# Later places for the casts of the middle parts of the last two tiles in a fused attention kernel

## What is computed

```
q = (x @ wq).reshape(B, T, H, D)          # B=16, T=512, H=16, D=16
lat = x @ w_down
k = (lat @ wk_up).reshape(B, T, H, D)
v = (lat @ wv_up).reshape(B, T, H, D)
q = _apply_rope(q, cos, sin)
k = _apply_rope(k, cos, sin)
scores = jnp.einsum('bqhd,bkhd->bhqk', q, k) * scale
scores = jnp.where(allowed[None, None], scores, jnp.finfo(scores.dtype).min)
attn = jax.nn.softmax(scores, axis=-1)
out = jnp.einsum('bhqk,bkhd->bqhd', attn, v).reshape(B, T, E)
return out @ wo
```

## Time and profile before

| | |
|---|---|
| median of 3 runs | 1903.85 us |
| lowest, highest | 1903.59, 1912.81 us |
| the profiled execution, its own time | 1909.18 us |
| its span, first to last instruction | 1907.3 us |
| attention turns with the changed table | about 640 to 1290 us of the span |
| one full turn | 47.1 us |

### The profile page before, as it was taken

How to read it: one execution, slowest core, us unless ns; L and a number is a source line. 1 busy time by engine, 2 the same in 40 slices (tenths; PEclk the granted TensorE clock), 3 DMA queues, 4 the chain that set the end, 5 groups by cost and what they waited for, 6 DMA issues and landing times. The chain is left out here.

```text
span 1907.3 us, 32059 instructions
## 1 busy us (share of the span) xinstructions
PE 1791.9 (94%) x10553; PEld 1102.0 (58%) x10554; DVE 1311.0 (69%) x3400; ACT 1124.8 (59%) x2292; POOL 843.5 (44%) x923
## 2 busy tenths in 40 slices
PE   6999999999957799999999999999799999989997
PEld 3666666777733355555555555555456666667776
DVE  4777776566638577777777777777277777756664
ACT  5777775125424667777777777777477777721111
POOL 1111101777746666566655555550011111147776
PEclk9999999999977899999999999999899999999999
DMA  2424341999933333333333333332222433249996
GB/s 77 128 84 142 95 131 56 264 258 258 260 77 94 95 100 103 101 102 101 102 101 102 101 101 102 90 90 58 66 86 73 129 108 123 80 143 261 263 259 145
DMA packets 192287, 243.72 MB, mean 128 GB/s; under 512 B 17559, under 2 KB 159607, under 8 KB 192126
## 3 DMA queue, kind: packets, MB, share of 16 engines
q1 hardware_dynamic: 166286, 202.62, 35.0%
q0 software_dynamic: 24576, 37.77, 10.3%
q10 hardware_dynamic: 1264, 1.31, 0.2%
HBM read 126.65 MB, written 63.86 MB: 100 GB/s over the span
## 5 line engine op out<-in xcount | busy, mean ns | idle before, releaser
L1403 DVE TENSOR_REDUCE a_smax<-a_p_ring 128x1 f32<-128x512 f32 (+2 forms) x768 | 355.2, 506 | 134.1 <-PE a_p_ring L1494 128.5
L1302 ACT ACTIVATE a_probs<-a_p_ring 128x512 f32<-128x512 f32 x640 | 368.2, 607 | 109.0 <-PE a_p_ring L1506 107.7
L1494 PE MATMUL a_p_ring<-p_ks,p_qs 100*128 100x512 bf16 (+3 forms) x1024 | 246.6, 307 | 16.3 <-ACT a_smaxT L1339 5.5
L1506 PE MATMUL a_p_ring<-p_qs,p_ks 103*128 103x512 bf16 (+3 forms) x1024 | 243.4, 304 | 6.7 <-ACT a_probs L1302 5.8
L50 POOL TENSOR_TENSOR f_rstd<-f_mv,eps 128x4 f32<-128x4 f32 x31 | 14.8, 478 | 497.8 <-DVE f_mv L44 495.5
L676 ACT ACTIVATE e_silu<-e_p_up 128x176 f32<-128x176 f32 x128 | 40.6, 318 | 313.0 <-PE e_p_up L768 313.0
L519 PE MATMUL f_p_up<-f_xnT,ws1T 128*128 128x512 f32 x384 | 187.4, 611 | 1.1 <-ACT f_xnT L300 1.1
L1522 PE MATMUL a_p_out<-a_probs,p_v 128*32 128x512 f32 (+3 forms) x2048 | 177.6, 448 | 6.1 <-ACT a_probs L1302 6.1
L561 PE MATMUL f_p_z<-ws2T,f_hidden 128*128 128x256 f32 (+1 forms) x768 | 180.6, 384 | 0.7 <-DVE f_hidden L397 0.7
L137 POOL DMA_INDIRECT h_got<-rows,slot_token x128 | 125.8, 983 | 123.9 <-DVE slot_token L496 83.0
L519 PE MATMUL f_p_up<-f_xnT,ws3T 128*128 128x512 f32 x384 | 180.5, 592 | 0.0
(11 more groups left out here) (171 smaller groups left out, 3613.8 us busy)
## 6 DMA issues: line engine op xcount, KB each, us to landing
h_w<-w_in SPq DMA_DIRECT2D x128, 352.0 KB
p_qs<-a_parts SPq DMA_DIRECT2D x192, 128.0 KB, 2.4
p_ks<-a_parts SPq DMA_DIRECT2D x192, 128.0 KB, 2.4
h_w<-w_in SPq DMA_DIRECT2D x128, 176.0 KB
rows<-first_row SPq DMA_DIRECT2D x16, 640.0 KB, 6.4
rows<-f_row SPq DMA_DIRECT2D x16, 640.0 KB, 6.6
x<-x_in SPq DMA_DIRECT2D x16, 512.0 KB, 5.7
acc<-x SPq DMA_DIRECT2D x16, 512.0 KB, 3.3
```

Source lines behind the costliest of these rows:

```text
L1302: nc.scalar.activation(to[:], p_score[s][:], ACT.Exp, scale=SCALE).then_inc(score_free[s], 1)
L1403: ins = nc.vector.tensor_reduce(smax[:, t, 4 * g + h:4 * g + h + 1], p_score[s][:, at:at + length], AX.X, ALU.max)
L1494: ins = nc.tensor.matmul(p_score[s][:, at:at + length], qs[1 - u][0:SR + MASK, 4 * g + h, t * P:(t + 1) * P], ks[1 - u][0:SR + MASK, 4 * g ...
L1506: ins = nc.tensor.matmul(p_score[s][:, at:at + length], ks[u][0:SR + MASK + TOP, 4 * g + h, t * P:(t + 1) * P], qs[u][0:SR + MASK + TOP, 4 ...
```

## The change

Two numbers of the table `PROJECT` are different; no instruction is added or taken away.

```diff
-           (0.61, ("HIGH", 2)), (0.69, ("HIGH", 3)), (0.74, ("SPLIT", 2)), (0.765, ("SPLIT", 3))]
+           (0.61, ("HIGH", 2)), (0.69, ("HIGH", 3)), (0.80, ("SPLIT", 2)), (0.855, ("SPLIT", 3))]
```

## The result

| | before | with the change |
|---|---|---|
| median of 7 runs | 1903.85 us | 1897.39 us |
| lowest, highest | 1903.48, 1912.81 | 1893.53, 1901.79 |
| ratio to before, 95% interval | | 0.9957, 0.9940 to 0.9974 |
| profiled execution, its span | 1907.3 us | 1891.7 us |
| a full turn, mean of six | 47.19 us | 46.60 us |

The kernel became faster by 0.43% by the ratio (0.34% by the medians), and the interval leaves out no change. The forecast was 1896.4 us, 0.39% less, in a range of 1890 to 1904.5. The two profiled spans differ by 15.6 us, twice the difference of the medians. So the turns are read first, and what lies outside them is accounted for further down.

The account below looks back on a forecast made before the run. TensorE was taken to bound each attention turn, lengthened by two waits for ScalarE. Twelve turns at 0.53 us plus 1.07 us for sequence 13 gave 7.4 us: 1903.85 to 1896.4 us, range 1890 to 1904.5.

Parts of the forecast that it names:

- The bound: Attention turn: TensorE, busy 46.07 of 47.05 us, sets its length; others matter only through two TensorE waits, together 1.23 us.
- The first wait goes: TensorE's score product waiting for ScalarE's copy into `smaxT` no longer waits, starting 0.52 us earlier each full turn.
- `probs4` gains 0.53 us, the second wait stays: `probs4` starts 0.53 us earlier; TensorE's score product waiting for its bank still loses about 0.70 us a turn.
- One sign missed: Expected in the new profile's TensorE list over 13 turns: the wait for `probs` stays at about 4.4 us.
- case B: Rival: TensorE's wait merely moves to the bank of `probs7` or the product with V; time 1903.9 us, chance 0.13.
- The cast of tile 3 costs nothing behind `probs5`: On ScalarE the moved cast leaves `probs6` and `probs7` at their old moments, covered by 0.7 us of slack.
- The low parts, the maxima's parts and the DMAs: GpSimd's low parts end by 954.1 and 956.0, maxima's parts are not pushed, no SyncE DMA starts later.
- Sequence 13: Turn without normalisations, where the cast of tile 2 waited 0.69 us for GpSimd: `probs4` and TensorE gain 1.07 us.
- Sequence 0: Turn whose TensorE waits around the moved casts are for GpSimd: gain zero, at most 0.5 us.
- case C: Rival: a new TensorE idle gap in sequence 0 returns the full clock a stretch later; 1906.0 us, chance 0.04.
- The sum: Whole kernel: 12 full turns at 0.53 us make 6.36 us, plus 1.07 for the last sequence, 7.4 us.
- case A: Rival: both TensorE waits on ScalarE go, 1.23 us a turn, 16.3 us in all; time 1887.6 us, chance 0.09.

## Why the prediction was right

**The bound.** TensorE sets the turn, and the waits by bank were the two places at which ScalarE could lengthen it. Right in all experiments but one: with the last two normalisations late a third place came, the product with V.

**The first wait goes.** The copy into `smaxT0` starts 0.49 behind `probs0` and TensorE's product is in its stream. Right: the row is gone from the list of waits.

**`probs4` gains 0.53 us, the second wait stays.** The step on which the sum stands. The way to `probs4` shrank by 4.44 - 3.86 = 0.58 us, and the turn by 0.59. The second wait cost 0.68 us where 0.70 was worked out. The term was short by 0.05 us a turn, and the prices of ScalarE's steps show where: I took 0.48 or 0.49 us for each from rows in which casts stand between, and the steps around the copy were shorter once no cast was next to it. In the second profile with the change, whose mark is at 943.40, the copy starts 0.97 us and `probs1` 1.43 us behind the mark, where 0.99 and 1.47 were worked out:

```profile
943.89 0.63 ACT L1302 ACTIVATE a_probs<-a_p_ring 128x512 f32<-128x512 f32 x1
944.37 0.56 ACT L1339 COPY a_smaxT<-a_p_ring 24x512 bf16<-24x512 bf16 x1
944.83 1.53 ACT L1302 ACTIVATE a_probs<-a_p_ring 128x512 f32<-128x512 f32 x3
```

So 0.04 of the 0.05 us stand at `probs1` already.

The six turns measured were alike, but not all twelve are. In sequence 3 the cast of tile 2 waited for GpSimd before, as in sequence 13, and its turn gained 0.86 us (from 855.05 - 807.92 = 47.13 to 849.96 - 803.69 = 46.27 us); the other eleven gained 0.58 us on average. The sum took all twelve as sequence 6.

**One sign missed.** The wait for `probs` was to stay at about 4.4 us in the list and stands at 6.4. It took in the small waits ahead of it, which the prediction priced together with it (0.71 us) and did not add to the listed time. It did not grow by what the other wait lost (5.5 us), so case B did not come.

**The cast of tile 3 costs nothing behind `probs5`.** Right; the run with that cast even later gave the same turn within 0.02 us. The slack was worked out as 0.7 us, and the prediction's own figures (956.8 less 955.8) give 1.0. With the change `probs7` ended at 949.48 and the product with V behind it began 1.06 us later:

```profile
950.54 1.50 PE L1522 MATMUL a_p_out<-a_probs,p_v 128*32 128x384 f32 x24
```

**The low parts, the maxima's parts and the DMAs.** Right. GpSimd's two low parts ended at 947.78 and 949.75, and SyncE's DMAs started at 950.42, directly behind the score product at 950.01, as these rows of POOL and of SyncE show:

```profile
946.63 1.15 POOL L1265 TENSOR_TENSOR a_parts<-a_qk,a_parts 128x512 bf16<-128x512 f32 x1 [1.46 <-ACT a_parts L1351]
948.59 1.16 POOL L1265 TENSOR_TENSOR a_parts<-a_qk,a_parts 128x512 bf16<-128x512 f32 x1 [0.80 <-ACT a_parts L1351]
```

```profile
950.42 3.84 SPq L1146 DMA_DIRECT2D p_qs<-a_parts  x6
```

**The casts' inputs.** This was said too lightly, in case B: that both inputs were ready. The second input had 0.4 us to spare (951.41 against 951.82), the first none: it came just when the cast's place came up, as the run with the normalisation moved alone showed. It did no harm to the forecast, because the change moves that cast away from GpSimd; it would have spoilt a forecast for almost any other change to ScalarE ahead of it. My reading that ScalarE "starts one instruction behind the other without a gap" was true, and it did not show that only ScalarE's own length held it. The row of GpSimd at 949.14 and the wait in the turn of sequence 3 could have told.

**Sequence 13.** 1.07 us worked out. From the mark to the score product that waits: 1284.45 - 1279.38 = 5.07 us before, and with the change 1273.05 - 1269.03 = 4.02 us, by these rows, the first of them of the kernel before:

```profile
1279.38 0.38 PE L1560 MATMUL a_p_ring<-p_ident,p_smax_parts 128*128 128x128 bf16 x4
```

```profile
1269.03 0.38 PE L1560 MATMUL a_p_ring<-p_ident,p_smax_parts 128*128 128x128 bf16 x4
...
1273.05 0.39 PE L1506 MATMUL a_p_ring<-p_qs,p_ks 103*128 103x384 bf16 x2 [0.34 <-ACT a_probs L1302]
```

That is 1.05 us.

**Sequence 0 and case C.** From this turn's mark to the next transpose `MAX` were 18.63 us before (666.93 to 685.56) and 18.13 us with the change (664.34 to 682.47). The 0.5 us is the upper end that was allowed. That the casts gave it is not shown: 0.41 us of it lie in TensorE's four transposes of `OUT`, 4.5 us behind the mark. The first row is of the kernel before, the second with the change:

```profile
671.42 1.06 PE L1533 MATMUL a_p_ring<-ident,a_outT 128*128 128x128 f32 x4
```

```profile
668.79 0.60 PE L1533 MATMUL a_p_ring<-ident,a_outT 128*128 128x128 f32 x4
```

From their start to the next instruction were 0.85 us before and 0.44 us with the change, and 0.44 to 0.49 us in all eleven experiments, among them the one that moved only the last normalisation. In the kernel before they fall into the stretch of the low clock, 0.50 up to 672.5 us. It was profiled once, so whether the casts have a part in this is open. The clock did not return later; with the change the same stretch of the span has 0.72 in place of 0.50:

```profile
664.00:672.50 8.50, 8.16 (x60) 3.41 (x60) 5.33 (x13) 3.92 (x8) 4.69 (x5) 0.72 0.10 25
```

Case C, that it returns a stretch later, did not come in any of the runs. Its account of the low clock was too simple as well. It names the idle time ahead of 666.93, and the clock had fallen before that: in the kernel before the granted clock is 1.00 from 652 to 655 us and 0.50 from 656 to 664 us, after TensorE had waited 0.76 us ahead of 653.33 and 0.60 us ahead of 655.23.

**The sum.** Twelve turns gave 7.25 us by the marks of sequences 1 and 13 (713.37 to 1279.38 is 566.01 us, 710.27 to 1269.03 is 558.76 us), and sequence 13 gave 1.05: 8.3 us, where 7.4 was forecast. Of the 0.9 us between, 0.6 are the 0.05 us a turn and 0.3 are sequence 3. The difference of the medians is 6.5 us, and 8.2 us by the ratio (0.43% of 1903.85). That the median of 1897.39 came within 1.0 us of the forecast is luck: the seven runs before lie at 1903.5 to 1903.9 us (four) and 1910.1 to 1912.8 us (three), and with one more high run in place of a low one their median would have been 1910.1. The turns bear the prediction out, not the whole time.

**Where the 15.6 us of the two profiles lie.** 8.3 us are the changed turns, 0.5 us sequence 0. 2.6 us are there at the mark of sequence 0 (666.93 against 664.34), before any moved cast of these turns. About 4.2 us lie behind sequence 13, in the last feed-forward layer. The first lie ahead of every moved instruction, and nothing shows that the second come of the change: in the eleven profiles of the experiments the first transpose `MAX` came between 599.4 and 607.2 us, and the profile with both casts behind `probs4` at 0.86 and 0.92 took 632.4 us from the mark of sequence 13 to the end, 4.5 us more than before, with turns that were 1.1 us shorter. Longer times go with a lower granted clock: the 23 executions of the kernel before on one chip go from 1899.9 us at a mean of 0.981 to 1916.8 us at 0.971. What lowers the clock in one execution and not in the next is open.

**The chances.** Cases A, B and C did not come. What case A would have given, 1.23 us a turn, nearly came (1.12) once the cast of tile 2 had left the way to `probs4` too; the argument against A was that it had not.

## What to carry to other kernels

When a chain of one engine holds another, find the instruction at its end that the other waits for, and count what stands ahead of it: moving work from one place to another ahead of it changes which wait is listed and hardly the time (0.07 us of a turn here). A wait that disappears from a list is no gain until the next one on the same path has been priced; here the kernel that kept the listed wait was faster by 0.45 us a turn than the one that lost it. An engine that runs without a gap may still be held by another one whose results arrive just in time, so look up when each input was finished, in the rows of the engine that makes it, and look through all turns for one in which the wait shows; a run that takes something out settles it.

## What was not expected of the hardware

- An input that arrives exactly at its instruction's place leaves no idle time in that engine's rows: the cast of tile 2 had none ahead of it in sequence 6 of the kernel before (950.33), and the same start, 1.00 to 1.01 us behind the mark, in two kernels that had a normalisation less ahead of it.
- Behind the last transpose `MAX` (1329.26 us before) all thirteen kernels have the same instructions in the same order, and they took between 573.0 and 584.9 us, at a mean granted clock of 0.97 to 0.98 over the profiles. This scatter is larger than the effect of the change, while turns of the attention repeat within 0.02 us of a mean of six.
